# A decoder layer on one core: the first normalisation applied on features-by-tokens data by GpSimd, in place of TensorE transposes

## What is computed

```
x = x + selfattn(layernorm(x))   # blocks of 128 tokens, causal, one head of 512, softmax
x = x + crossattn(layernorm(x))  # 16 heads of 32, 64 context keys, silu(masked scores) in place of softmax
x = x + ffn(layernorm(x))        # 512 -> 2048 -> 512, exact gelu
layernorm(x) = (x - mean) / sqrt(var + 1e-5), without scale or shift
```

## Time and profile before

| | |
|---|---|
| three runs | 1313.2, 1313.33, 1313.77 us |
| the profiled execution: span from first to last instruction | 1312.2 us |
| its own time (the span and what lies around it) | not listed apart; the runs are 1.0 to 1.6 us above its span |
| attention part, about | 43 to 584 us of the span; one full step 64.77 us (queries end at 294.40 and at 359.17) |
| TensorE (PE) busy | 1289.4 us, 98% |
| DVE, ACT, POOL busy | 45%, 37%, 19% |
| mean granted clock of TensorE | 0.996 of full speed |

### The profile page before, as it was taken

The page is one execution under the profiler, slowest core; times in us unless marked ns, Lnnn a source line. Parts: engine busy times, 40 slices in busy tenths (PEclk is TensorE's granted clock), DMA queues, the critical chain, the costliest instruction groups (busy, mean ns, idle before and its releaser), DMA issues.

```text
span 1312.2 us, 15758 instructions
## 1 busy us (share of the span) xinstructions
PE 1289.4 (98%) x5897; PEld 1046.8 (80%) x5897; DVE 585.1 (45%) x1098; ACT 488.4 (37%) x887; POOL 244.2 (19%) x225
## 2 busy tenths in 40 slices
PE   9989999999999999999999999999999999999999
PEld 7877878787878788767888888888888888888887
DVE  7475768585858585845522222222312211222211
ACT  6254554545454555443322222222222222222221
POOL 1303232313141414138500100100102001001000
PEclk9998999999999999999999999999999999999999
DMA  8220202020202020316210010010010100100000
GB/s 288 73 72 0 85 1 84 1 85 0 84 0 84 0 84 4 116 42 208 64 65 0 0 65 1 0 64 0 25 39 0 64 0 0 64 0 0 32 0 32
DMA packets 40486, 60.04 MB, mean 46 GB/s; under 512 B 4224, under 2 KB 14464, under 8 KB 40448
## 3 DMA queue, kind: packets, MB, share of 16 engines
q1 hardware_dynamic: 40448, 59.53, 13.6%
HBM read 41.17 MB, written 18.35 MB: 45 GB/s over the span
## 4 chain that ended last, share of the span: by engine, by line
PE 54%; DMA 1%; DVE 0%; SPq 0%; ACT 0%; issue 0%; DVEq 0%
PE bank L50 18%; PE bank L51 18%; PE bank L49 18%; PE bank L140 1%; DMA w_raw<-in_w 0%; DMA x_dram<-resid 0%; DVE resid L1129 0%; SPq L1026 0%; DVE w_parts L184 0%; ACT w_parts L180 0%; SPq L1024 0%; SPq L1023 0%; SPq L188 0%; DVEq L1128 0%; SPq L1033 0%
## 5 line engine op out<-in xcount | busy, mean ns | idle before, releaser
L1121 DVE TENSOR_TENSOR hid_lo<-gelu_out,hid_hi 128x512 fp32r<-128x512 f32 x128 | 97.0, 758 | 493.7 <-ACT gelu_out L1097 493.7
L49 PE MATMUL bank<-zT,w_parts 128*128 128x512 f32 x768 | 300.9, 392 | 5.3 <-DVE zT L149 1.8
L51 PE MATMUL bank<-zT,w_parts 128*128 128x512 f32 x768 | 301.1, 392 | 0.0
L50 PE MATMUL bank<-zT,w_parts 128*128 128x512 f32 x768 | 301.0, 392 | 0.0
L1093 ACT ACTIVATE hid_hi<-bank,b_col 128x512 fp32r<-128x512 f32 x128 | 88.0, 688 | 484.4 <-PE bank L51 484.4
L49 PE MATMUL bank<-w2p_hi,hid_lo 128*128 128x512 f32 x512 | 203.8, 398 | 0.7 <-DVE hid_lo L1121 0.7
L50 PE MATMUL bank<-w2p_lo,hid_hi 128*128 128x512 f32 x512 | 202.5, 395 | 0.0
L51 PE MATMUL bank<-w2p_hi,hid_hi 128*128 128x512 f32 x512 | 202.4, 395 | 0.0
L49 PEld LDWEIGHTS bank<-zT,w_parts 128*128 128x128 f32 x768 | 145.1, 189 | 39.5 <-issue 3.0
L50 PEld LDWEIGHTS bank<-zT,w_parts 128*128 128x128 f32 x768 | 144.8, 189 | 32.1
L51 PEld LDWEIGHTS bank<-zT,w_parts 128*128 128x128 f32 x768 | 144.8, 189 | 31.0
(11 more groups left out here) (138 smaller groups left out, 1816.6 us busy)
## 6 DMA issues: line engine op xcount, KB each, us to landing
x_in<-in_x SPq DMA_DIRECT2D x32, 256.0 KB, 3.4
x_dram<-resid SPq DMA_DIRECT2D x32, 256.0 KB, 2.1
w_raw<-in_w SPq DMA_DIRECT2D x32, 256.0 KB, 3.4
resid<-x_dram SPq DMA_DIRECT2D x32, 256.0 KB, 3.1
out_dram<-resid SPq DMA_DIRECT2D x32, 256.0 KB, 2.1
resid<-in_wqkvT SPq DMA_DIRECT2D x12, 256.0 KB, 4.2
mask_i<-in_mask SPq DMA_DIRECT2D x16, 128.0 KB, 2.6
values_now<-values_dram SPq DMA_DIRECT2D x8, 256.0 KB, 2.8
```

The lines of the kernel that those rows point to most:

```text
L49: pe.matmul(out_ap, lhs[1], rhs[0], start=start, stop=False)
L50: pe.matmul(out_ap, lhs[0], rhs[1], start=False, stop=False)
L51: return pe.matmul(out_ap, lhs[0], rhs[0], start=False, stop=stop)
L1121: dve.tensor_tensor(hid[1][:, c % 4, :], gelu_out[:, c % 2, :], f(hid[0][:, c % 4, :]), ALU.subtract).then_inc(hid_lo, 1)
```

## The change

The first normalisation of tiles 1 to 7 no longer goes through `zn` and TensorE. x comes a second time in a layout of features by tokens (`xT`, laid out before the launch, 1 MB a tile) into a new tile `x_cols`. The means and reciprocal deviations of the 512 tokens are computed a tile ahead, stored to DRAM as two rows of 512 numbers (`norms_dram`), and loaded back spread over all 128 partitions (`norm_cols`). POOL subtracts and multiplies. ACT and DVE then split `x_cols` into `zT` directly. Tile 0 keeps the old way in the setup.

In step (a, b), with `more(a)` true for a = 0 to 6:

- **SP** gets `load_ahead(a)` in front of everything else: four loads of x rows of tile a + 1 into two buffers of `w1_raw` (256 KB each), the 1 MB load of `x_cols`, the two stores of 512 numbers each, and the load of `norm_cols` (512 KB). It waits there for the statistics, for z1T_lo, for the aggregate, for the reciprocal deviations (`ln1[3]`) and for both stores. `load_kv`, `load_mask`, `load_x` and `store_x2` follow it.
- **TensorE** loses the 16 transposes; y goes to banks 0 to 3 and waits for `q_lo` of the same chunk as well; cross scores m wait for `q_lo` of chunk m only (before: 2m + 2 chunk halves, that is chunk 1 for m = 0 and chunk 3 for m = 1). The other banks are dealt anew with the same pattern of reuse.
- **ACT** copies from `x_cols` (`z1_high`) in place of `chunk_high`.
- **DVE** loses the four `zn` rows and the aggregate in `start_step`; `z1_low` takes the place of `chunk_low`; two row statistics (`stats_ahead`) stand between `mask_scores(3)` and y_low, and two more with the aggregate of tile a + 1 stand behind the scaling of `prob` and before v_low and o_low. In step 7 the four statistics for the third normalisation stand behind the last second residual, before `last_step`.
- **POOL** takes `norm_rstd` of tile a + 1 behind `silu_low(7)`, and behind `norm_rstd` of the second normalisation the four subtractions and four multiplications.
- DVE and POOL are peeled by 2 like SP, and the scratch space for DMA descriptors is set to 2048 bytes.

```diff
-VALUE_BANK = (1, 2, 3, 4)
-SELF_BANK = (0, 7)
-KEY_BANK = (3, 4)
-SCORE_BANK = (0, 1, 2, 3, 5, 6, 7, 0)
-OUT_BANK = (3, 4, 5, 1)
-BLOCK_BANK = (6, 7, 0, 2)
-PROJ_BANK = (3, 4, 5, 1)
+VALUE_BANK = (5, 6, 7, 0)
+SELF_BANK = (4, 3)
+PROB_BANK = 5
+KEY_BANK = (7, 0)
+SCORE_BANK = (4, 5, 6, 7, 1, 2, 3, 4)
+OUT_BANK = (7, 0, 1, 5)
+BLOCK_BANK = (2, 3, 4, 6)
...
+    def load_ahead(a):
+        n = a + 1
+        for i in range(NB):
+            sp.wait_ge(ln1[0], NB * n + (i // 2) * (i - 1))
+            sp.dma_start(ahead(i), x_blocks[n * NB + i, :, :]
+                         ).then_inc(ahead_loaded[i % 2], 16)
+            if i == 1:
+                if not first(a):
+                    sp.wait_ge(z1T_lo, EC * n)
+                sp.dma_start(x_cols[:, :, :], xT[n, :, :, :]).then_inc(cols_loaded, 16)
+        sp.wait_ge(ln1[1], NB * (n + 1))
+        with nc.allow_non_contiguous_dma(reason="a column of norms becomes a row"):
+            sp.dma_start(norms_dram[n, 0, :, :].rearrange("i p -> p i"), mv1[:, :, 0]
+                         ).then_inc(norms_stored, 16)
+            sp.wait_ge(ln1[3], n + 1)
+            sp.dma_start(norms_dram[n, 1, :, :].rearrange("i p -> p i"), rstd1[:, :]
+                         ).then_inc(norms_stored, 16)
+        sp.wait_ge(norms_stored, 32 * n)
+        if not first(a):
+            sp.wait_ge(z1_scaled, EC * a)
+        sp.dma_start(norm_cols[:, :, :].rearrange("p s t -> p (s t)"),
+                     norms_dram[n, :, :, :].rearrange("s i p -> (s i p)").partition_broadcast(P)
+                     ).then_inc(norms_loaded, 16)
     def step(a, b, par):
+        if more(a):
+            load_ahead(a)
         if b is not None:
             sp.wait_ge(kv_ready, len(BLOCKS) * (b + 1))
             load_kv(b + 1)
...
@@ -543,11 +582,12 @@
     def step(a, b, par):
         if b is not None:
-            norm_rstd(pool, mv1, ve1, rstd1, ln1, a)
             for j in range(4):
                 silu_low(b, j)
-        pool.wait_ge(z1_ready, NB * (a + 1))
-        for i in range(NB):
+        else:
+            pool.wait_ge(z1_ready, NB)
+        for i in range(NB):
+            pool.wait_ge(x_loaded[i], 16 * (a + 1))
             pool.tensor_tensor(x_in[:, i, :], x_in[:, i, :], bout_row[:, :], ALU.add
                                ).then_inc(x_biased, 1)
         if b is not None:
@@ -557,20 +597,32 @@
             for c in range(EC):
                 pool.tensor_tensor(wo[1][:, c, :], raw(WO_CHUNK + c), f(wo[0][:, c, :]),
                                    ALU.subtract).then_inc(wo_lo, 1)
+        if more(a):
+            norm_rstd(pool, mv1, ve1, rstd1, ln1, a + 1)
         norm_rstd(pool, mv2, ve2, rstd2, ln2, a)
+        if more(a):
+            pool.wait_ge(cols_loaded, 16 * (a + 1))
+            pool.wait_ge(norms_loaded, 16 * (a + 1))
+            for c in range(EC):
+                pool.tensor_tensor(x_cols[:, c, :], x_cols[:, c, :], norm_cols[:, 0, :],
+                                   ALU.subtract).then_inc(z1_centred, 1)
+            for c in range(EC):
+                pool.wait_ge(z1_centred, EC * a + c + 1)
+                pool.tensor_tensor(x_cols[:, c, :], x_cols[:, c, :], norm_cols[:, 1, :],
+                                   ALU.mult).then_inc(z1_scaled, 1)
     def last_step(b):
         norm_rstd(pool, mv3, ve3, rstd3, ln3, 0)
         for j in range(PAIRS):
...
             keys_high(b)
             for m in range(EC):
                 q_high(b, m)
             for c in range(EC):
-                chunk_high(act, a, c, 4)
+                z1_high(b, c)
             for j in range(4):
                 silu(b, j)
...
-    def start_step(b, mv, rstd, ln, t):
-        dve.wait_ge(ln1[0], NB * (b + 2))
+    def aggregate(n, mv, ln):
+        dve.wait_ge(ln1[0], NB * (n + 1))
         dve.nop(nofuse=True)
         for i in range(NB):
             dve.bn_aggr(mv[:, i, :], stats1[:, i, :]).then_inc(ln[1], 1)
+    def stats_ahead(a, blocks):
+        for i in blocks:
+            dve.wait_ge(ahead_loaded[i % 2], 32 * a + 16 * (i // 2 + 1))
+            dve.nop(nofuse=True)
+            dve.bn_stats(stats1[:, i, :], ahead(i)).then_inc(ln1[0], 1)
+    def start_step(b):
         dve.wait_ge(mask_loaded, 32 * (b + 1))
         dve.tensor_scalar(mask_f[:, :], mask_i[:, :], 0.0, None, ALU.not_equal
                           ).then_inc(mask_ready, 1)
-        for rows in (first(b), not first(b)):
-            if rows:
-                dve.wait_ge(z2T_done, NB * (b + 1))
-                norm_rows(dve, lambda i: x_in[:, i, :], mv, rstd, ln, t)
-            else:
-                dve.wait_ge(kv_hi, len(SECOND + BLOCKS) * (b + 1))
-                for (hi, lo), source in BLOCKS:
-                    dve.tensor_tensor(lo, source, f(hi), ALU.subtract).then_inc(kv_ready, 1)
+        dve.wait_ge(kv_hi, len(SECOND + BLOCKS) * (b + 1))
+        for (hi, lo), source in BLOCKS:
+            dve.tensor_tensor(lo, source, f(hi), ALU.subtract).then_inc(kv_ready, 1)
+    def z1_low(a, c):
+        dve.wait_ge(z1T_hi, EC * a + c + 1)
+        dve.tensor_tensor(zT[1][:, c, :], x_cols[:, c, :], f(zT[0][:, c, :]), ALU.subtract
+                          ).then_inc(z1T_lo, 1)
     def step(a, b, par):
         if b is not None:
-            start_step(b, mv1, rstd1, ln1, a)
+            start_step(b)
             for m in range(EC):
                 q_low(b, m)
             for c in range(EC):
-                chunk_low(dve, a, c, 4)
+                z1_low(a, c)
             dve.wait_ge(mask_ready, b + 1)
             for j in range(4):
                 mask_scores(b, j)
+        if more(a):
+            stats_ahead(a, (0, 1))
         for m in range(EC):
-            low(yv, m, 4 + m, y_hi, y_lo, EC * a + m + 1)
+            low(yv, m, m, y_hi, y_lo, EC * a + m + 1)
         for i in range(NB):
             if i % 2 == 0:
                 dve.wait_ge(s1_done, 2 * a + i // 2 + 1)
...
@@ -754,6 +820,9 @@
         for i in range(NB):
             dve.tensor_scalar(prob[:, i, :], prob[:, i, :], rden[:, i:i + 1], None, ALU.mult
                               ).then_inc(prob_ready, 1)
+        if more(a):
+            stats_ahead(a, (2, 3))
+            aggregate(a + 1, mv1, ln1)
         if b is not None:
             for i in range(2):
                 v_low(a, i)
...
@@ -788,22 +857,23 @@
         dve.nop(nofuse=True)
         for i in range(NB):
             dve.bn_aggr(mv2[:, i, :], stats[:, i, :]).then_inc(ln2[1], 1)
-        next_stats(dve, a + 1, (0, 1))
         norm_rows(dve, lambda i: x1_rows(i, par), mv2, rstd2, ln2, a)
         if b is not None:
             second_residual(b, 0, 1 - par)
             second_residual(b, 1, 1 - par)
-            next_stats(dve, a + 1, (2, 3))
             second_residual(b, 2, 1 - par)
         for i in range(NB):
             transpose_low(dve, i, BLOCK_BANK[i], z2T_hi, z2T_lo, a)
         if b is not None:
             second_residual(b, 3, 1 - par)
-        else:
-            next_stats(dve, a + 1, (2, 3))
+        if not more(a):
+            next_stats(dve, TILES, range(NB))
     def last_step(b):
-        start_step(b, mv3, rstd3, ln3, 0)
+        aggregate(TILES, mv3, ln3)
+        start_step(b)
+        dve.wait_ge(z2T_done, NB * (b + 1))
+        norm_rows(dve, lambda i: x_in[:, i, :], mv3, rstd3, ln3, 0)
         q_low(b, 0)
         q_low(b, 1)
         dve.wait_ge(mask_ready, b + 1)
...
         pe.wait_ge(z2T_lo, NB * (b + 1))
         for m in chunks_:
-            if m == 1 and not first(b):
+            if m < 2 and not first(b):
+                pe.wait_ge(x2_ready, NB * b - 2 + m)
+            project(m, lambda c: at(wq, c, cols(m)), lambda c: at(zT, c), q_done)
+    def step(a, b, par):
+        if b is not None:
+            queries(b, range(EC))
+            if not first(b):
                 pe.wait_ge(x2_ready, NB * b)
-            project(m, lambda c: at(wq, c, cols(m)), lambda c: at(zT, c), q_done)
-    def step(a, b, par):
-        if b is not None:
-            queries(b, range(EC))
-            transposed_chunks(pe, a, 4)
             pe.wait_ge(kv_ready, len(BLOCKS) * (b + 1))
             for m in range(2):
-                pe.wait_ge(q_lo, 2 * (EC * b + 2 * m + 2))
+                pe.wait_ge(q_lo, 2 * (EC * b + m + 1))
                 cross_scores(m)
         for m, c in [(m, 0) for m in range(EC)] + [(m, c) for m in range(EC)
                                                    for c in range(1, EC)]:
             if c == 0:
                 pe.wait_ge(z1T_lo, EC * a + m + 1)
-            last = product(pe, bank[4 + m][:, :], at(wqk, c, cols(m)), at(zT, c),
+                if b is not None:
+                    pe.wait_ge(q_lo, 2 * (EC * b + m + 1))
+            last = product(pe, bank[m][:, :], at(wqk, c, cols(m)), at(zT, c),
                            c == 0, c == EC - 1)
             if c == EC - 1:
                 last.then_inc(y_done, 1)
...
+        "xT": np.asarray(x).reshape(TILES, TILE, EC, P).transpose(0, 3, 2, 1)
```

(2 more changed lines are left out.)

33 lines of the change are left out of this document (24 added, 9 removed).

## The result

| | before | after |
|---|---|---|
| median of 4 runs | 1313.26 us | 1368.17 us |
| lowest and highest | 1312.19, 1313.77 | 1365.77, 1370.06 |
| ratio, 95% interval | | 1.0419 [1.0404, 1.0434] |
| profiled execution, its span | | 1368.34, 1366.6 us |

A forecast was written before the change was run, and what follows sets the result against it. It took TensorE, busy 98% of the span, as the bound; 3.5 us (tiles 2 to 6) plus 1.2 (tile 7) plus 0 (tile 1) less 1.3 (last step) gave 1313.3 - 3.4 = 1309.9 us, range 1306.8 to 1318.5.

The forecast's parts named there:

- SP and the DMAs: Between reciprocal deviations and first subtraction: store 2.5 us, broadcast 3.6 us, keys still landing in time; cost 0.
- Rival 1: POOL's centring beside key and value splits slows both, up to 2.0 us a tile, 1321.9 us; chance 0.16 for over 1316.
- rival 3: The new idle ahead of y brings TensorE's clock to half in six tiles, 16 us, 1326 us; chance 0.05.
- the gain of y: In tiles 2 to 7 y starts at 297.6 instead of 298.82, gaining 1.2 us a steady step.
- pv late: Second statistics pair and aggregate delay DVE by 1.7 us, so pv starts 0.5 us later in steps 1 to 6.
- the moved first pair of statistics: Two row statistics ahead of y_low, 1.2 us, fit in DVE's idle 1.70 us; cost 0.
- the transposes' 1.84 us: TensorE time of the 16 removed transposes per step, upper bound of the gain, most of it not obtained.
- 5 x (1.2 - 0.5): Sum for tiles 2 to 6: y's gain less pv's delay in each, 3.5 us together.
- value rows 2: Value rows waiting for o_low(0): their 0.25 us delay lies inside pv's delay, adding nothing.
- the last step: Four statistics ahead of the aggregate delay the last step by 1.0 us, plus 0.3 for low clock: cost 1.3 us.
- POOL, cost 0: POOL's `norm_rstd` and eight centring operations, 10.4 us, end before ACT needs them and cost nothing by themselves.
- the 0 for tile 1: In tile 1 an earlier y gains 0.5 us and a late pv loses 0.5: net 0.

The follow-up runs named there:

- k3: Changed kernel with the numbers laid out in DRAM partition by partition, reciprocal deviations stored as 128 rows of 16 bytes, POOL reading with a stride: 1320.72 us, ratio 1.0064.
- k2: Changed kernel with POOL making the next tile's reciprocal deviations ahead of `silu_low(4)` instead of behind `silu_low(7)`: 1327.62 us, ratio 1.0117.
- k4: Changed kernel with POOL's eight centring operations cut to one column each, all DMAs and waits kept: 1340.94 us, ratio 1.0220.
- k7: k2 with POOL also waiting for the rows of the second normalisation before centring: 1316.32 us, ratio 1.0027.
- k9: Changed kernel, numbers made early, one store in 16-byte rows; POOL subtracts behind `silu_low(7)`, multiplies behind the second normalisation's rows: 1312.38 us, ratio 0.9996.
- k10: k9 with the third normalisation's four statistics back at their old places: 1310.99 us, ratio 0.9986; run again 1312.00 us, ratio 0.9997.
- k1: Changed kernel with SP issuing the next step's keys and values ahead of the stores of the numbers: 1358.88 us, ratio 1.0352.
- k12: k10 with step 0's subtractions moved behind the second normalisation's `norm_rstd` and its rows: 1312.92 us, ratio 0.9999.

## Why the prediction was wrong

**The step that failed** is "SP and the DMAs", cost 0. It chose 2.5 us for the store between 1.7 and 3.4, "since the count is that of the upper row and the bytes those of the lower". Both bounds came from rows with packets of 64 and 512 bytes; at 4 bytes the store took 9.0, far above the upper one. The broadcast took 6.0 for 3.6, above its bound of 4.1 too. The numbers themselves were ready in time: 9.7 us ahead of the second transposes (288.46 for 298.18), forecast 9.4. So the first subtraction came 15.3 us behind them and not 6.4, and keys that were to land 2 us ahead of their need became 4.41 us of waiting on ACT. No row of the trace priced this store, which the text said. The nearest in the size of its pieces stood in the DMA view of the kernel before and weren't used: two 2 KB loads in 128 rows of 16 bytes, in a crowded queue, which would at least have raised the upper bound.

```profile
bk_col<-in_bk SPq DMA_DIRECT2D x1, 2.0 KB, 6.3
bq_col<-in_bq SPq DMA_DIRECT2D x1, 2.0 KB, 6.1
```

The text should then have worked out what a store of 7 or 10 us does, and SP's order gave that at once. That the store's length is the cause, and not only its company, is shown by k3, which changes the layout in DRAM and POOL's stride with it and has 47 of the 55 us back; k2, which takes the slow stores out of the way, has 41.

**The rule of the Trainium skill** pointed the right way. By DMA: Bandwidth & Descriptors of the Trainium skill (Rules for kernel authors, Specifications) a strided last dimension is one descriptor per element and under 512 B there is a read-modify-write. k3 agrees with the first half as to the direction, 9.0 against 1.4 us for the same bytes. For the second half no run speaks: the rows of 16 bytes are under 512 B as well, and were there in 1.4 us. The forecast had doubled the upper row to 6.8 us and got 1321 us. That was still far too low, as only the overlap was costed with it.

**Rival 1** named the right mechanism, and had chance 0.16 and a price capped at 2.0 us a tile. By its own rate, 0.7 us for each us of the two DMAs beyond 7.8, the measured 15 would have cost 5. It counted the contention alone. It left out that the keys stand behind the same store in SP's queue (k4: about half of the loss with POOL silent), and that what is lost ahead of y is lost as idle time of TensorE, which then works at the low clock for 10.2 us of each step (3.7 us lost). That is **rival 3**, which I took as a case of its own with chance 0.05, from the 1.2 us wait. The waits ahead of it were rival 1's. The two rivals weren't alternatives but a chain, and no rival stood for the sum.

**Right, shown by k2, k7 and k9:** the gain of y, 1.20 us (1.2); its wait of 0.88 us (about 1.2); pv late by 0.63 (0.5); no wait from the moved first pair of statistics; the transposes' 1.84 us not given back in full. No wait is put down to the new banks, but no run tests them alone. Step 7, which has no late pv, is 1.0 us shorter in k10's second run (63.75 for 64.77; 1.2).

**Too high by half, even with the store mended: "5 x (1.2 - 0.5)".** Steps 2 to 6 of k9 take 64.37, 64.64, 64.33, 64.39 and 64.33 us where they took 64.8, 1.8 us less together and not 3.5. In such a step y gains 1.20, pv loses 0.63 and the stretch behind the start of pv another 0.11. Only 0.3 of the 0.63 stands directly ahead of pv. 0.16 stands around value rows 2, which the forecast had put inside the other delay, and 0.11 behind the first matmul of y, which now starts after a wait.

**Right in kind: the last step.** The four statistics cost it 1.0 us of wait (3.9 us in k9, 2.9 in k10), as worked out, and the step 1.1 us (22.12 for 21.03).

**Wrong besides:** "POOL, cost 0". It was weighed against the key splits, in rival 1, from the 1.78 and 1.76 us of the earlier trace rows; against the rows of the second normalisation it wasn't, though these too read and write SBUF alone: 1.92 us became 5.78 in k2. (The eight splits, which rival 1 put at 6 us beside POOL, take 7.3 in k1.) With the store mended this is the next cost, and any earlier start of the centring meets it. And the 0 for tile 1: by the transposes of step 1 the kernel after was 4.0 us behind (153.42 for 149.42), with waits of 4.52 and 1.82 us ahead of its scores and y, because the keys came late through the same stores (as in k7). Steps 2 to 7 add 7.3 to 9.2 us each.

**What the forecast would have been** with those steps mended: k9 to k12 are the change with the store short and the centring moved off DVE's work, and stand at 0.9986 to 0.9999 of the kernel before. In their profiled executions they are 1.9 to 3.4 us ahead by the transposes of step 7, where the sum had 4.7, and 0.9 to 2.2 by the third normalisation, where it had 3.4. The medians of the spans show almost none of it. One reason is that the kernel before's own profiled span, 1312.2 us, lies 1.7 us above the median of its spans in the set of k9; another is the clock in the feed-forward part (last section). What else takes the rest is open.

## What to carry to other kernels

A transfer that no row of the trace prices is an open term, above all one of many tiny pieces: the forecast should say what happens at three times the guess, and walk down the issuing queue behind it. Work that is moved to POOL is free only where DVE isn't doing work of the kinds that were slowed here, with all its tensors in SBUF (normalised rows, key and value splits; row statistics weren't), at the same moment; each place where DVE has such work is a place to check, not only the nearest. And where TensorE is 98% busy, an extra wait of some microseconds can cost its own length and, behind it, a stretch at half clock; price the two as one. The wait of 0.88 us ahead of y in k2, k7 and k9 to k12 brought no such stretch in any steady step. Last, a wait at the start of a pipeline may be cover for one behind it: k9's 4.83 us in step 0 were won back by the transposes of step 1, k10's 4.52 all but 1 us, and k12, which removed it, met the next.
